# A graph-network kernel: the second graph layer's relu goes from VectorE to ScalarE, in two halves

## The reference

```
h = relu(einsum('ts,bsh->bth', adj, x @ Wg0 + bg0))
h = relu(einsum('ts,bsh->bth', adj, h @ Wg1 + bg1))     # the relu in question
for p in 1..4:                                           # MAX_SKIP = 4
    last = lstm_last(Wih[p-1], Whh[p-1], ..., windows of p nodes of h)
    h = h.at[:, every p-th node].set(last)
x = layernorm(x + h)
```

## Time and profile before

| | us |
|---|---|
| median of 3 runs | 624.95 (624.62 to 625.41) |
| the profiled execution | 624.48 |
| its span, first to last instruction | 622.7 |
| PE busy | 605.8 (97%) |
| VectorE busy | 473.1 (76%) |
| ScalarE busy | 434.3 (70%) |
| one of slots 3 to 7 (from a place in it to the same place in the next) | 56.09 |

### The profile page before, as it was taken

The page is one execution under the profiler, slowest core; times in us unless marked ns, Lnnn a source line. Parts: engine busy times, 40 slices in busy tenths (PEclk is TensorE's granted clock), DMA queues, the critical chain, the costliest instruction groups (busy, mean ns, idle before and its releaser), DMA issues.

```text
span 622.7 us, 9523 instructions
## 1 busy us (share of the span) xinstructions
PE 605.8 (97%) x2614; PEld 419.7 (67%) x2614; DVE 473.1 (76%) x1623; ACT 434.3 (70%) x1000; POOL 207.9 (33%) x324
## 2 busy tenths in 40 slices
PE   9999999999999999999999999999999999999994
PEld 5646556447875687578668757865885686576794
DVE  4999999876947767876878788778868876465666
ACT  3668776956947775795777668567947775556774
POOL 1365551005332043227404540740373064003301
PEclk9999999999999999999999999999999999999998
DMA  8334000000000010001001100100010010000000
GB/s 337 145 126 170 1 2 0 0 1 2 1 2 1 0 35 1 2 11 58 1 2 30 39 1 2 35 35 1 20 49 2 0 35 35 0 2 34 2 35 34
DMA packets 8981, 20.00 MB, mean 32 GB/s; under 512 B 2016, under 2 KB 5088, under 8 KB 8800
## 3 DMA queue, kind: packets, MB, share of 16 engines
q1 hardware_dynamic: 8928, 19.40, 8.7%
HBM read 12.05 MB, written 4.19 MB: 26 GB/s over the span
## 4 chain that ended last, share of the span: by engine, by line
PE 76%; ACT 4%; DVE 3%; issue 2%; POOL 1%; POOLq 0%; ACTq 0%; DVEq 0%
PE QQ L898 27%; PE QQ L910 15%; PE PA L881 4%; PE PA L853 4%; PE PB L872 2%; PE PB L863 2%; PE PB L731 2%; PE PA L731 2%; PE PA L833 2%; PE PB L833 2%; PE QQ L932 1%; PE PA L684 1%; PE PA L844 1%; PE PB L951 1%; PE QQ L942 1%
## 5 line engine op out<-in xcount | busy, mean ns | idle before, releaser
L1273 ACT ACTIVATE raw<-QQ,BL 128x256 f32<-128x256 f32 (+2 forms) x279 | 150.1, 558 | 69.6 <-PE QQ L898 36.9
L898 PE MATMUL QQ<-HT,WT 128*128 128x256 f32 (+2 forms) x558 | 183.5, 473 | 0.8 <-DVE HT L1792 0.4
L898 PEld LDWEIGHTS QQ<-HT,WT 128*128 128x128 f32 x558 | 103.9, 190 | 58.2 <-issue 29.7
L475 POOL TENSOR_TENSOR RSD<-VAR,pw 128x4 f32<-128x4 f32 (+1 forms) x43 | 61.8, 1437 | 175.9 <-DVE VAR L1498 175.5
L910 PE MATMUL QQ<-HB,WT 128*128 128x256 f32 (+2 forms) x336 | 100.8, 443 | 0.4 <-DVE HB L1792 0.2
L554 POOL COPY HB<-HB 32x256 f32<-32x256 f32 x96 | 42.9, 447 | 150.0 <-DVE HB L1685 144.8
L910 PEld LDWEIGHTS QQ<-HB,WT 128*128 128x128 f32 x336 | 61.1, 190 | 30.9 <-issue 13.4
L1309 ACT ACTIVATE raw<-raw 128x256 f32<-128x256 f32 (+4 forms) x79 | 37.1, 470 | 30.2 <-DVE raw L1774 25.8
L1764 DVE SCALAR_TENSOR_TENSOR raw<-raw 128x256 f32<-128x256 f32 (+2 forms) x60 | 31.6, 527 | 15.7 <-ACT raw L1273 15.1
L1792 DVE SCALAR_TENSOR_TENSOR HB<-raw 128x256 f32<-128x256 f32 (+4 forms) x42 | 20.3, 483 | 23.6 <-ACT raw L1309 23.6
L1108 ACT ACTIVATE X<-Z,OFF,RSD 128x128 f32<-128x128 f32 x80 | 31.8, 482 | 2.5 <-POOL OFF L481 2.5
(11 more groups left out here) (254 smaller groups left out, 1157.6 us busy)
## 6 DMA issues: line engine op xcount, KB each, us to landing
four<-in_x SPq DMA_DIRECT2D x8, 512.0 KB, 3.8
raw<-in_xt SPq DMA_DIRECT2D x8, 512.0 KB, 6.4
out<-four SPq DMA_DIRECT2D x7, 512.0 KB, 2.6
HB<-HB SPq DMA_DIRECT2D x96, 32.0 KB, 1.8
WT<-in_lstm SPq DMA_DIRECT2D x1, 2048.0 KB, 8.0
later<-in_later SPq DMA_DIRECT2D x1, 725.5 KB, 10.2
AD<-in_adj SPq DMA_DIRECT2D x2, 256.0 KB, 4.5
out<-four SPq DMA_DIRECT2D x2, 256.0 KB, 2.0
```

Source lines behind the costliest of these rows:

```text
L475: pool.tensor_tensor(RSD[kk][:, ts], VAR[kk][:, ts], pw[:, ts], ALU.pow).then_inc(ln[k]["rstd"], some)
L898: mm = pe.matmul(steps_view(Q[q], k), WT[:, 0, (p - 1) * 4 + q, :], ht_view(par, k), start=True, stop=(s == 0))
L1273: act.activation(TG[q][:, at:n], Q[q][:, at:n], ACT.Tanh, scale=0.5 if q == G else 0.25, bias=BL[:, p - 1, q:q + 1]).then_inc(g_ok, 1)
```

## The change

The `a_hidden` of VectorE is no longer called in slots 2 to 7 (it stays in slot 8). ScalarE gets an `a_hidden` with an argument h for the half: half 0 reads the first bank of PA and stands between gates(8) and state(8); half 1 reads the second bank and stands behind `a_mixed(s, (0,1))`, ahead of gates(9). Each half adds one to `h1_ok`, and PE's mix 1 now waits for the first half alone (2g - 1), mix 3 for both.

```
-                    reach(pe, h1_ok if b % 2 else y1_ok, 2 * g)
+                    reach(pe, h1_ok, 2 * g - 1 + b // 2) if b % 2 else reach(pe, y1_ok, 2 * g)
...
+            def a_hidden(g, par, h):
+
+                act.wait_ge(h1_ps, halves(g, h))
+                reach(act, ht_ps, g - 1)
+                act.activation(by_batch(HT[:, par])[:, 2 * h:2 * h + 2], PA[:, part(h)].rearrange("p (b n) -> p b n", n=NODES),
+                               ACT.Relu, scale=2.0).then_inc(h1_ok, 1)
...
-                cell(8)
-                a_mixed(s, (0, 1)) if A else None
+                gates(8)
+                a_hidden(s - 1, 1 - par, 0) if A else None
+                state(8)
+                if A:
+                    a_mixed(s, (0, 1))
+                    a_hidden(s - 1, 1 - par, 1)
...
-                if A:
-                    a_turn_blocks(s, (3,))
-                    a_hidden(s - 1, 1 - par)
+                a_turn_blocks(s, (3,)) if A else None
                 cell(8)
```

## The result

| | before | after |
|---|---|---|
| median of the runs | 624.81 us (624.46 to 625.46, 22 runs) | 625.9 us (625.49 to 628.5, 22 runs) |
| ratio after / before | | 1.0018 (1.0012 to 1.0024) |
| a second set (e9_again, with 29 runs of the kernel before) | 624.87 us | 625.7 us (10 runs), 1.0014 (1.0005 to 1.0023) |
| one slot | 56.09 us | 56.09 us (56.25 from a place in slot 3 to the same in slot 4) |
| VectorE / ScalarE busy | 473.1 / 434.3 us | 464.0 / 446.6 us |

The changed kernel is slower by about 1.1 us. The time lies inside the range given, but the sum was wrong: it said no change, and there is a small, real one. That it lies inside is luck: the upper end of the range was taken from a third of the price of late ScalarE halves, and the halves were not late.

A forecast was written before the change was run, and what follows sets the result against it. The prediction took PE's own instruction stream as the bound. Every term was 0 in each of six slots, so 624.48 us stayed for the profiled execution, 624.9 us as median, range 623.8 to 626.3.

The forecast's parts named there:

- the range given: Whole kernel's median time: 623.8 to 626.3 us, meant to hold 8 in 10.
- the sum: Whole kernel: six slots times 0 - 0 + 0 + 0 on 624.48 us, so no change; 624.9 us as median.
- late ScalarE halves: ScalarE between gates(8) and gates(9): longer halves delay PE by 0.61 us a slot, 3.7 in six, 628.6 us; chance 0.11.
- What bounds the kernel: Slots: PE's own instruction stream is the bound; other engines count only through its gaps or by making a new one.
- Removed relu, 0: VectorE, six slots: 1.98 us each, 11.9 us of work, goes; PE gains 0, as freed time is not carried on.
- A half, 1.09 us: ScalarE: each relu half takes 1.09 us, as the same instruction does in the start-up.
- Half 0 and the tanh of step 8: ScalarE behind gates(8): first half ends at 340.36, 0.61 us before mix 1 needs it; tanh starts 0.79 us earlier; cost 0.
- Half 1: ScalarE before gates(9): second half runs 342.63 to 343.72, fitting the idle time with 0.15 us to spare; cost 0.
- The second projection's 0.22 us: PE's second projection: its weight load still waits 0.22 us for ScalarE's copy of line 1214, since mix 1 does not move.
- A slot's length: Slots: each still lasts 56.09 us; a change of over 0.2 us would make the prediction wrong.
- The faster rivals: PE's weight-load wait at the second projection closes, 623.6 us, chance 0.06; or VectorE's load counts fully, 613.1 us, chance 0.01.
- The bound on "same": Whole kernel: a measurement can tell about 0.2%, 1.25 us, from no change; same was given 0.83.

The follow-up runs named there:

- e9_again: The changed kernel, unaltered, run and profiled once more: 625.7 us (10 runs), ratio 1.0014 to the kernel before.
- e7_order_before: The kernel before, relu still on VectorE, with PE's second projection put behind h(9) in slots 2 to 7: 623.27 us, ratio 0.9972.
- e4_both: The changed kernel with both relu halves between gates(8) and state(8) on ScalarE, PE's mix 1 waiting for both: 627.1 us, ratio 1.0033.
- e1_refill: The changed kernel with 12 already-reached wait instructions put back into VectorE's queue, two per slot where the relu had stood: 625.04 us, ratio 1.0001.
- e3_shift116: The kernel before, relu still on VectorE, with 116 already-reached wait instructions added to VectorE's queue in slots 2 to 7: 625.54 us, ratio 1.0011.

## Why the prediction was wrong, point by point

- *What bounds the kernel:* right. PE is busy for 280.86 of 281.00 us of the slots, and a wait of a few tenths of a microsecond that reached it was paid nearly in full late in the span (0.34 and 0.35 of 0.36) and by 0.15 of 0.36 behind slot 3.
- *Removed relu, 0:* right for its work. VectorE lost 9.2 us of busy time, not 12 (in the slots' stretch 7.6, where five relus give 9.9): the group of each step's first product grew from 26.4 to 27.4 us there, and instructions of one engine overlap a little, so that the relu had covered ends of others (337.82 against 337.90). None of it reached PE.
- *A half, 1.09 us:* right. Group by line of the kernel after, count and min/median/max:

```profile
L1259 ACT ACTIVATE HT<-PA x12: 1095/1101/1108, 227.0 to 511.0; 128x512 f32<-128x512 f32 x12
```

- *Half 0 and the tanh of step 8:* right. ScalarE's idle time before the tanh went from 1.88 us to nothing. It started at 340.39, where 340.36 + 0.20 was forecast on this profile's times; it may start before the half has ended. Half 1 fits: 0.24 us were left before gates(9), forecast 0.15.
- *The second projection's 0.22 us stays:* right. A slot's length: right, 56.09 us; only from slot 3 to slot 4 is it 56.25, by a pause. The faster rivals did not happen; the gap had to be closed in PE's order (e7_order_before), not by an earlier ScalarE.
- *The slower rival, late halves:* did not happen; e4_both shows its place and its deadline right, and two halves in a row 0.27 us sooner done than by adding durations.
- *The sum, 0:* **wrong, and this is the step that failed.** It held the instructions, durations and waits of the six slots, and I let "the freed time is not carried on" stand for "nothing is carried on". What is carried on is a count: VectorE's queue is 12 instructions shorter for everything behind, and the places at which it pauses for 0.36 us move with it. In the kernel after three of them fall on waits whose end PE is waiting for: 0.15 + 0.34 + 0.35 us, with 0.10 in the last lane, where ScalarE's longer queue has such a place, 0.94 of the 1.0 us by which the spans differ. e1_refill took it away without touching the change, e3_shift116 brought it without the change.
- *The bound on "same":* the table of 22 runs told 0.18% from nothing; the loss is 1.1 us.

That the pauses lie on a grid of 128 instructions, show where VectorE has just stood at a wait, and cost 0.36 us is shown. Their cause was only argued: about 0.67 us after the start of the delayed instruction a packet of 8192 bytes starts in a DMA queue of the kind "instruction" (552.50 and 553.18 before; 558.44 and 559.13, 601.00 and 601.68 after), which would be 128 instructions of 64 bytes; that looks like the queue's own refill. The count of the packets fits. The pages of the kernel before and of e3_shift116 have

```profile
q14 instruction: 32, 0.26, 0.1%
```

```profile
q14 instruction: 33, 0.27, 0.1%
```

(packets, MB, share). VectorE's queue has 16 numbers that are 63 above a multiple of 128, ScalarE's 12, GpSimd's 3 and SyncE's 1, which is 32; e3_shift116 has one more, 2111 on VectorE. So the packets go with these numbers; that the engine stands still because of the refill is still an inference. The Trainium skill, "Runtime: NRT & Kernel Launch", section "Instruction fetch mechanics", says that engines stream their instructions in blocks of 16 KiB (256 instructions) and that crossing a block is mostly hidden. The 64 bytes agree with the packets. The block agrees for TensorE, whose 5431 instructions are 21.2 times 256 and beside which the page of the profile has 21 packets of 16384 bytes ("q8 instruction: 21, 0.34, 0.2%"); for VectorE and ScalarE the distance here is 128. And hidden it is only where nobody waits. No run here varied the size of the packets, or separated the refill from another cause with the same spacing.

## What to carry to other kernels

A change that costs nothing where it stands can still move a long queue by some instructions, and with it pauses of a few tenths of a microsecond. Where TensorE has no slack, as here, three such pauses made 1 us, so a bound of that size belongs to a change of the instruction count, and an A/B test of a small edit should be repeated with the count restored. Compare the traces instruction by instruction for offset against the kernel before; the steps in that offset, not the busy sums, show where the time went. And look first for what is out of order on the bound engine itself: one projection behind one group of matmuls gave 1.6 us, where moving 12 us of work between two engines with slack gave none.

## What was not expected of the hardware

- VectorE's pause: 0.36 us at instruction 63 above a multiple of 128, counting waits as instructions, seen at 703, 1087, 959, 1855, 1983 and 2111, each in at least one of the kernels. Where VectorE was still busy there, no delay is seen.
- Two waits of `past` make one instruction in the queue, and 116 such instructions in six slots cost next to nothing by themselves (behind its start-up, e3_shift116 loses 0.08 us in the slots up to 559 us, and the rest at its two pauses).
- TensorE's start: in one execution of the changed kernel the warm-up matmuls and the next ones ran 0.8 and 2.1 us longer, and neighbouring matmuls of line 661 were about 0.85 us apart until 10.6 us instead of 0.43. That is a ratio of two, as between the two levels of 1.2 and 2.4 GHz, but the clock column reads 1.00 for the first 8 us in this trace as in that of the kernel before, so the level itself is not shown. This execution was 2.6 us above its median. What decided it is open.
- ScalarE's instructions overlapped where nothing was waited for: the first half started 0.11 us before the gates ahead of it had ended, and the tanh 0.09 us before the half. Two halves in a row overlapped more: of 1.10 and 1.15 us, they took 2.02 us together (e4_both).
